# New places for the pieces of eight batches in the order lists of four engines

## The chip, the cores and the metric

The kernel runs on one core of one Trainium2 chip. The metric is device time in microseconds (us), the median of the runs; lower is better. The core's engines work through instruction lists of their own, in order, and meet at semaphores: TensorE (PE), VectorE (DVE), ScalarE (ACT), GpSimd (POOL) and SyncE (SP), which here only issues DMAs.

## What is computed

Eight batches of 512 rows with 256 features, in float32, pass through an attention block and a feed-forward block with experts:

```python
x = x + layernorm(attention(layernorm(x)))      # 16 heads of 16
x = x + layernorm(ffn(layernorm(x)))            # 8 experts, width 1024

# attention: the softmax weights are summed against the row's own v
att = softmax(einsum('blhd,bmhd->blmh', q, k) * scale, axis=2)
opt = einsum('blmh,blhd->blhd', att, v)
# ffn: the expert of a row is the argmax of its gate logits
base = x @ wi.T + wi_b
out = sum over i of (expert == i) * (relu(base + lora_i(x)) @ wo.T + wo_b)
```

In this form of attention a row's weights are summed over the keys before they meet v, so all that is needed of the 512x512 scores of a head is the exponentials' sum (divided by itself). The kernel still computes all scores, their maxima and exponentials.

## The kernel before

**Pieces.** A batch has 16 heads of 512 queries in four tiles of 128: 64 scores of 128x512. Score i is one matmul into one of NS = 5 PSUM banks `ps` (line 227); DVE takes its row maximum (`maximum`, line 735); ACT takes the exponential in place, with its sum (`exponential`, line 523). Score i waits until exponential i - 5 is done, since it uses its bank. The three remaining banks `pu` go round among all other pieces: `take` gives the next bank and waits until the last user of it has been evicted.

Around the scores lie, for batch b + 1: statistics (`x_stats`, DVE) and norm of x (`x_norm`, POOL), its transposes (`x_t`), the projections q, k (`q_k`, four pieces of six matmuls, in the order 0, 2, 1, 3) and v (`value`); each product is of float32 numbers split in a high and a low part, three matmuls. ACT evicts the high part, DVE forms the low one. For batch b - 1: the ratio of the sums (`ratio`, `ratio_whole`, DVE), `scale` of v (POOL), `o_t`, `project`, `y_stats`, `y_norm`, `sum_stats`, `sum_norm`, `y_t`, the gate (`gate`, `gate_t`, `logits`, `gate_1` to `gate_3`, `mask`, `masked_t`) and the first products of the feed-forward block, `f1` (eight pieces; f1_lows on POOL splits the first six, f1_last on DVE the last two). For batch b - 2: the end of f1, `f2` (eight pieces of twelve matmuls), `y2_bias`, `y2_stats`, `y2_norm`, and the store.

**Order.** The order is written out by hand. In each engine's function, `slot(s)` stands for score s + 4 on the PE, maximum s + 2 on DVE and exponential s on ACT, and the other pieces stand between the slots. Before the change one list serves batches 0 to 6 (pieces of batches that don't exist do nothing) and one serves batch 7, where the second half of the rows is finished in halves (`o_half`, `y_half`, `gate_half`, `f1_half`, `f2_last`) after the last score. In batches 0 and 1 the PE runs one idle matmul on `ones_r` (line 206) ahead of each score whose number isn't in FULL.

**Transfers.** q and k of each head have to lie on other partitions for the scores: `stacks(b, j)` on SP issues eight DMAs from qk to `stack` (line 1202) for piece j, a quarter of a batch, into a ring of three; `first_piece` does so in halves at the start, on SP and POOL. q_k(b + 1, 0) on ACT waits until all stacks of batch b have landed, for it overwrites qk. In batch 0 SP also loads weights in stages into buffers used otherwise later: it waits for late 4 (POOL has split the first half of wi), then issues the second half of wi, the lora weights and stacks(0, 2), waits for late 12 (wo split), then issues x of batches 2 and 3 and stacks(0, 3).

```python
            for b in range(B):
                if b:
                    stacks(b, 3)
                store(b - 3)
                load_x(b + 2 if b >= 2 else B)
                stacks(b + 1, 0), stacks(b + 1, 1), stacks(b + 1, 2)
```

## Time and profile before

| | us |
|---|---|
| median of 3 runs | 535.78 (535.15 to 537.13) |
| span of the profiled execution | 533.9 |
| DVE, ACT, POOL busy in it | 467.3, 454.1, 344.7 |
| PE busy, modelled | 509.3 |
| exponential 0 of batch 0 | 23.25 |
| exponential 0 of batches 1, 2 and 7 | 72.02, 132.33, 427.41 |

The span begins with the first instruction. Matmuls overlap and their ends are modelled, so a busy PE isn't a full one. "Idle before <- releaser" in a timeline row is the time that the engine stood still ahead of the instruction, and what released it. In a chain row a piece is on the path that ended last; ACT's exponentials count there as two instructions each, the exponential and the read of its sum.

### The profile page before, as it was taken

The page shows a single profiled execution, that of the slowest core. Times are in us where ns is not written, and L with a number is a line of the kernel's source. Part 1 is how long each engine was busy: PE and PEld are TensorE (multiplying, and loading weights), DVE is VectorE, ACT ScalarE, POOL GpSimd, SP SyncE. Part 2 cuts the span into 40 slices and gives each one's busy share as a digit, 9 for nine tenths or more (in the row PEclk, how much of TensorE's full clock was granted, in tenths as well). Part 3 has the DMA queues.
Part 4 walks back from the last instruction along what each step waited for, and adds up shares of the span by engine and source line. Part 5 has one row for each costly group of instructions (what it writes and reads, how often), then busy time and mean ns, then how long its engine had stood idle before and what let it go on. Part 6 is the DMA issues. An engine that isn't in the chain of part 4 may idle for free.

```text
span 533.9 us, 8929 instructions
## 1 busy us (share of the span) xinstructions
PE 509.3 (95%) x2752; PEld 412.8 (77%) x2752; DVE 467.3 (88%) x1005; ACT 454.1 (85%) x1238; POOL 344.7 (65%) x544
## 2 busy tenths in 40 slices
PE   8899989899999999999999999999999999899995
PEld 6666645688897779877897779877887778677995
...
GB/s 233 194 239 112 95 143 80 1 34 170 63 89 1 146 93 152 6 68 170 50 111 1 160 79 158 1 100 137 111 9 16 174 163 5 80 41 1 1 40 41
DMA packets 22691, 47.63 MB, mean 89 GB/s; under 512 B 5266, under 2 KB 13586, under 8 KB 22004
## 3 DMA queue, kind: packets, MB, share of 16 engines
...
q0 software_dynamic: 256, 0.52, 0.4%
q8 instruction: 22, 0.36, 0.3%
q10 hardware_dynamic: 432, 0.59, 0.3%
q14 instruction: 25, 0.20, 0.1%
...
## 4 chain that ended last, share of the span: by engine, by line
PE 52%; ACT 30%; POOL 6%; SPq 4%; DVE 3%; issue 2%; DMA 1%; POOLq 0%; ACTq 0%
PE pu L199 25%; ACT ps L523 22%; PE ps L227 10%; PE pu L283 5%; SPq L1202 3%; ACT y L590 3%; PE pu L239 3%; PE ps L199 2%; PE ps L206 2%; POOL y L1032 2%; DMA stack<-qk 1%; POOL nmr L1026 1%; PE pu L305 1%; ACT qk L537 1%; POOL xb L1038 1%
## 5 line engine op out<-in xcount | busy, mean ns | idle before, releaser
L523 ACT ACTIVATE ps<-ps,nmax 128x512 f32<-128x512 f32 x512 | 346.2, 705 | 19.8 <-DVE nmax L735 19.6
L735 DVE TENSOR_REDUCE nmax<-ps 128x1 f32<-128x512 f32 x512 | 324.5, 681 | 25.9 <-PE ps L227 24.3
L227 PE MATMUL ps<-stack 128*128 128x512 f32 x512 | 186.7, 420 | 2.3 <-ACT ps L523 1.6
L523 ACT ACTIVATION_READ_ACCUMULATOR ps<-ps,nmax 128x1 f32 x512 | 129.4, 253 | 0.0
L227 PEld LDWEIGHTS ps<-stack 128*128 128x128 f32 x512 | 93.5, 190 | 27.1 <-ACT ps L523 12.5
L199 PEld LDWEIGHTS pu<-wo_r,inter 128*128 128x128 f32 x744 | 95.4, 188 | 3.8
L199 PE MATMUL pu<-wo_r,inter 128*128 128x256 f32 x744 | 97.2, 282 | 0.0
L199 PE MATMUL pu<-yT,wi_r 128*128 128x512 f32 x336 | 87.4, 395 | 0.0
L199 PEld LDWEIGHTS pu<-yT,wi_r 128*128 128x128 f32 x336 | 63.2, 188 | 14.0 <-ACT xn L590 0.2
L206 PE MATMUL ps<-ones_r 128*128 128x512 f32 x132 | 55.1, 459 | 7.7 <-ACT ps L523 6.5
L1046 POOL TENSOR_TENSOR ml<-gs,g 128x128 f32<-128x128 f32 (+1 forms) x9 | 3.5, 387 | 77.9 <-DVE g L887 77.9
L199 PE MATMUL pu<-xnT,wqk_r 128*128 128x512 f32 x192 | 49.6, 396 | 0.8 <-DVE xnT L739 0.7
L206 PEld LDWEIGHTS ps<-ones_r 128*128 128x128 f32 x132 | 26.4, 202 | 30.7 <-ACT ps L523 24.4
L1103 POOL TENSOR_TENSOR inter<-y,inter 128x1024 fp32r<-128x1024 f32 x19 | 45.4, 2390 | 1.5
L199 PEld LDWEIGHTS pu<-xnT,wqk_r 128*128 128x128 f32 x192 | 35.5, 188 | 10.0 <-ACT y L635 1.2
L1026 POOL TENSOR_TENSOR nmr<-nmr,halves 128x2 f32<-128x2 f32 (+2 forms) x50 | 39.8, 797 | 4.2
L1038 POOL TENSOR_TENSOR xb<-xb,y 128x256 f32<-128x256 f32 x58 | 41.1, 735 | 1.8
L1069 POOL TENSOR_TENSOR vo<-vo,sone 128x256 f32<-128x256 f32 x32 | 18.9, 622 | 30.8 <-DVE sone L838 26.5
L283 PE MATMUL pu<-wout_s,oT 128*128 128x256 f32 x120 | 31.2, 384 | 3.1 <-ACT oT L551 2.1
L1023 POOL TENSOR_SCALAR nmr<-mv 128x2 f32<-128x2 f32 (+2 forms) x50 | 12.0, 240 | 34.0 <-DVE mv L782 30.9
L1032 POOL TENSOR_SCALAR y<-y,nmr 128x256 f32<-128x256 f32 x58 | 31.6, 555 | 2.4
L283 PEld LDWEIGHTS pu<-wout_s,oT 128*128 128x128 f32 x120 | 22.1, 189 | 9.4 <-issue 5.4
...
## 6 DMA issues: line engine op xcount, KB each, us to landing
stack<-qk SPq DMA_DIRECT2D x256, 128.0 KB, 2.5
...
```

The lines of the kernel that those rows point to most:

```text
L199: p = e.matmul(out_, lT(a, c), r(b_, c), start=first and n == 0 and j == 0, stop=last and n == len(chunks) - 1 and j == 2)
L206: e.matmul(bank[:].rearrange("p (k m) -> p k m", k=4), ones_r[:], ones_r[:].unsqueeze(1).to_broadcast([128, 4, 128]), start=True, stop=True)
L227: e.matmul(ps[i % NS][:], st[:, 1 - p, c, t * 128:(t + 1) * 128], st[:, 2, c, :], start=True, stop=True).then_inc(scored, 1)
L239: p = e.transpose(bank[:, t * 128:(t + 1) * 128], src[:, t, c * 128:(c + 1) * 128], id_s[:])
L283: p = e.matmul(o, oT[:, c, t * 128:(t + 1) * 128], wout_s[:, c, :], start=c == 0, stop=c == 1)
L523: e.activation(ps[i % NS][:], ps[i % NS][:], ACT.Exp, bias=nmax[:, i % 8:i % 8 + 1], accum_out=ssum[:, b % 2, t, h:h + 1]).then_inc(exped, 1)
L735: e.tensor_reduce(nmax[:, i % 8:i % 8 + 1], ps[i % NS][:], AX_X, ALU.max, negate=True).then_inc(maxed, 1)
L1026: e.tensor_tensor(nmr[n][:, 2, s], nmr[n][:, 1, s], halves[:, s], ALU.pow).then_inc(rstd[i], 1)
L1032: e.tensor_scalar(dst[:, t, :], src[:, t, :], nmr[n][:, 0, t:t + 1], nmr[n][:, 2, t:t + 1], ALU.add, ALU.mult).then_inc(normed[i], 1)
L1038: e.tensor_tensor(xb[:, b % XB, t, :], xb[:, b % XB, t, :], src[:, t, :], ALU.add).then_inc(added[i], 1)
L1069: e.tensor_tensor(vt, vt, sone[:, t, :].unsqueeze(2).to_broadcast([128, H, 16]), ALU.mult).then_inc(scaled, 1)
L1103: e.tensor_tensor(inter[:, 1, f:f + 2, :], whole, high.bitcast(F32), ALU.subtract).then_inc(f1_pool_low, 1)
```

## The change

The order lists of PE, ACT and DVE are written out anew, as four: batch 0, batch 1, batches 2 to 6, and batch 7. POOL has batch 1 apart. No piece is added or left out but one idle matmul (FULL has 30 numbers, not 31). Some moves: in middle batches f1(b - 1, 4) is evicted at the start of the next batch; f2 starts four scores later; q_k(b + 1, 3) goes from slots 40, 43 and 44 to slots 46, 49 and 49 of PE, ACT and DVE; in batch 0, x_t(1, .) comes earlier and value(1, .) and q_k(1, 3) later. x_stats(1) stands ahead of the first maximum, and x_norm(1) ahead of the splits of wi and wo on POOL. Four waits for loaded weights go from the start of batch 1 to the pieces that read them: wout_loaded to project(0, 0), late to gate(0), lora_moved to f1(0, 0), bg_loaded to gate(0) on ACT. SP's list is unchanged.

The old lists, which the diff takes away, are in the kernel above. Of the new ones the diff shows those of PE, ACT and DVE for the middle batches, the start and parts of batches 0, 1 and 7, and POOL's.

```diff
 
 
-IDLE, FULL = (25, 6, 4), (20, 29, 32, 35, 38, 41, 43, 45, 68, 70, 71, 72, 74, 84, 90, 93, 96, 97, 99, 102, 105,
-                           107, 109, 111, 112, 113, 115, 120, 123, 126, 127)
+IDLE, FULL = (25, 6, 4), (8, 28, 32, 35, 39, 50, 53, 61, 69, 71, 73, 75, 76, 82, 84, 90, 96, 98, 99, 100, 102, 103,
+                           105, 107, 109, 112, 115, 117, 121, 126)
 NS = 5
...
             def project(b, t):
                 if here(b):
                     u, k = divmod(t, 2)
+                    if b == 0 and t == 0:
+                        e.wait_ge(wout_loaded, 16)
...
                     bank = banks[take(("gate", b), gT_here, b + 1)]
+                    if b == 0:
+                        e.wait_ge(late, LATE)
                     e.wait_ge(yT_low, 2 * b + 2)
...
                           (0, 1), True, False)
                     if f == 0:
+                        if b == 0:
+                            e.wait_ge(lora_moved, 16)
                         e.wait_ge(lt_here, b + 1)
...
@@ tensor @@
...
+            def slot(s):
+                score(2 * PAIRS * b + s + 4)
+
+            b = 0
+            slot(0), slot(1), slot(2), slot(3), slot(4), slot(5), slot(6), slot(7), x_t(b + 1, 0), x_t(b + 1, 1)
+            slot(8), slot(9), slot(10), slot(11), slot(12), slot(13), slot(14), slot(15), slot(16), slot(17)
+            slot(18), slot(19), slot(20), slot(21), slot(22), slot(23), slot(24), slot(25), slot(26), slot(27)
+            q_k(b + 1, 0), slot(28), slot(29), slot(30), slot(31), q_k(b + 1, 2), slot(32), slot(33), slot(34)
+            q_k(b + 1, 1), slot(35), slot(36), slot(37), slot(38), q_k(b + 1, 3), slot(39), slot(40), slot(41)
+            slot(42), slot(43), slot(44), slot(45), slot(46), slot(47), slot(48), slot(49), value(b + 1, 0)
+            slot(50), slot(51), slot(52), value(b + 1, 1), value(b + 1, 2), slot(53), slot(54), slot(55), slot(56)
+            slot(57), slot(58), slot(59), slot(60), value(b + 1, 3), slot(61), slot(62), slot(63)
+
...
+            for b in range(2, B - 1):
+                slot(0), slot(1), slot(2), f1(b - 2, 7), slot(3), slot(4), o_t(b - 1, 0), o_t(b - 1, 1), slot(5)
+                slot(6), slot(7), project(b - 1, 0), slot(8), slot(9), project(b - 1, 1), slot(10), slot(11)
+                project(b - 1, 2), project(b - 1, 3), slot(12), slot(13), slot(14), slot(15), f2(b - 2, 0, 0)
+                slot(16), f2(b - 2, 0, 1), slot(17), slot(18), f2(b - 2, 1, 0), slot(19), slot(20), f2(b - 2, 1, 1)
+                slot(21), slot(22), x_t(b + 1, 0), slot(23), x_t(b + 1, 1), slot(24), slot(25), f2(b - 2, 2, 0)
+                slot(26), slot(27), f2(b - 2, 2, 1), slot(28), slot(29), slot(30), f2(b - 2, 3, 0), slot(31)
+                slot(32), f2(b - 2, 3, 1), y_t(b - 1, 0), y_t(b - 1, 1), slot(33), slot(34), q_k(b + 1, 0), slot(35)
+                slot(36), gate(b - 1), slot(37), q_k(b + 1, 2), slot(38), slot(39), gate_t(b - 1), slot(40)
+                value(b + 1, 0), slot(41), value(b + 1, 1), slot(42), value(b + 1, 2), slot(43), q_k(b + 1, 1)
+                slot(44), slot(45), slot(46), value(b + 1, 3), q_k(b + 1, 3), slot(47), slot(48), slot(49)
+                masked_t(b - 1), slot(50), f1(b - 1, 0), slot(51), f1(b - 1, 1), slot(52), slot(53), f1(b - 1, 2)
+                slot(54), slot(55), slot(56), f1(b - 1, 3), slot(57), slot(58), slot(59), slot(60), f1(b - 1, 4)
+                slot(61), slot(62), f1(b - 1, 5), slot(63), f1(b - 1, 6)
+            b = B - 1
+            slot(0), slot(1), slot(2), f1(b - 2, 7), slot(3), o_t(b - 1, 0), o_t(b - 1, 1), slot(4), slot(5)
+            slot(6), project(b - 1, 0), project(b - 1, 1), slot(7), slot(8), slot(9), project(b - 1, 2), slot(10)
+            project(b - 1, 3), slot(11), slot(12), f2(b - 2, 0, 0), slot(13), f2(b - 2, 0, 1), slot(14), slot(15)
+            slot(16), slot(17), f2(b - 2, 1, 0), slot(18), slot(19), slot(20), f2(b - 2, 1, 1), slot(21)
+            f2(b - 2, 2, 0), slot(22), slot(23), slot(24), slot(25), f2(b - 2, 2, 1), slot(26), slot(27)
+            y_t(b - 1, 0), slot(28), y_t(b - 1, 1), slot(29), slot(30), f2(b - 2, 3, 0), gate(b - 1), slot(31)
+            slot(32), slot(33), gate_t(b - 1), f2(b - 2, 3, 1), slot(34), o_half(0), slot(35), slot(36), slot(37)
+            project(b, 0), slot(38), masked_t(b - 1), slot(39), project(b, 1), slot(40), slot(41), f1(b - 1, 0)
+            slot(42), slot(43), slot(44), f1(b - 1, 1), slot(45), f1(b - 1, 2), slot(46), slot(47), slot(48)
+            slot(49), f1(b - 1, 3), slot(50), slot(51), slot(52), f1(b - 1, 4), slot(53), slot(54), slot(55)
+            f1(b - 1, 5), slot(56), f1(b - 1, 6), slot(57), slot(58), slot(59), f1(b - 1, 7), f2(b - 1, 0, 0)
+            more_banks(), f2(b - 1, 0, 1), o_half(1), project(b, 2), project(b, 3), y_half(0), f2(b - 1, 1, 0)
+            f2(b - 1, 1, 1), gate_half(0), f2(b - 1, 2, 0), gate_t_half(0), f2(b - 1, 2, 1), f2(b - 1, 3, 0)
+            y_half(1), f2(b - 1, 3, 1), masked_t_half(0), gate_half(1), f1_half(0, 0), gate_t_half(1), f1_half(0, 1)
+            f1_half(0, 2), f1_half(0, 3), masked_t_half(1), f1_half(1, 0), f1_half(1, 1), f2_last(0), f1_half(1, 2)
+            f1_half(1, 3), f2_last(1), f2_last(2), f2_last(3)
 
...
 
             def gate(b):
                 if here(b):
+                    if b == 0:
+                        e.wait_ge(bg_loaded, 16)
...
@@ scalar @@
...
+            b = 0
+            slot(0), slot(1), slot(2), slot(3), slot(4), slot(5), slot(6), slot(7), slot(8), slot(9), slot(10)
+            slot(11), slot(12), slot(13), slot(14), x_t(b + 1, 0), x_t(b + 1, 1), slot(15), slot(16), slot(17)
+            slot(18), slot(19), slot(20), slot(21), slot(22), slot(23), slot(24), slot(25), slot(26), slot(27)
+            slot(28), slot(29), slot(30), slot(31), q_k(b + 1, 0), slot(32), slot(33), slot(34), slot(35)
+            q_k(b + 1, 2), slot(36), slot(37), slot(38), q_k(b + 1, 1), slot(39), slot(40), slot(41), slot(42)
+            slot(43), slot(44), slot(45), slot(46), slot(47), slot(48), slot(49), slot(50), slot(51), q_k(b + 1, 3)
+            slot(52), slot(53), slot(54), slot(55), slot(56), slot(57), slot(58), slot(59), slot(60), slot(61)
+            slot(62), slot(63), value(b + 1, 0), value(b + 1, 1)
...
+            for b in range(2, B - 1):
+                f1(b - 2, 4), slot(0), slot(1), f1(b - 2, 5), slot(2), f1(b - 2, 6), slot(3), slot(4), slot(5)
+                slot(6), f1(b - 2, 7), o_t(b - 1, 0), o_t(b - 1, 1), slot(7), slot(8), slot(9), slot(10), slot(11)
+                slot(12), slot(13), slot(14), slot(15), slot(16), slot(17), slot(18), slot(19), slot(20), slot(21)
+                slot(22), slot(23), slot(24), f2(b - 2, 0), slot(25), slot(26), slot(27), x_t(b + 1, 0), slot(28)
+                slot(29), x_t(b + 1, 1), slot(30), slot(31), slot(32), slot(33), slot(34), f2(b - 2, 1)
+                y_t(b - 1, 0), y_t(b - 1, 1), slot(35), slot(36), q_k(b + 1, 0), slot(37), slot(38), gate(b - 1)
+                slot(39), q_k(b + 1, 2), slot(40), slot(41), logits(b - 1), slot(42), slot(43), value(b + 1, 0)
+                gate_exp(b - 1), slot(44), slot(45), slot(46), q_k(b + 1, 1), slot(47), value(b + 1, 1), slot(48)
+                slot(49), q_k(b + 1, 3), masked_t(b - 1), slot(50), slot(51), f1(b - 1, 0), slot(52), slot(53)
+                slot(54), slot(55), f1(b - 1, 1), slot(56), slot(57), slot(58), slot(59), slot(60), f1(b - 1, 2)
+                slot(61), f1(b - 1, 3), slot(62), slot(63)
...
@@ vector @@
...
+            x_stats(1)
             maximum(0), maximum(1)
...
+            slot(28), slot(29), slot(30), slot(31), slot(32), slot(33), slot(34), slot(35), q_k(b + 1, 0), slot(36)
+            slot(37), slot(38), q_k(b + 1, 2), slot(39), slot(40), slot(41), slot(42), slot(43), slot(44), slot(45)
+            slot(46), slot(47), slot(48), slot(49), slot(50), slot(51), q_k(b + 1, 1), slot(52), slot(53)
...
+            b = 1
+            ratio(b - 1), slot(0), ratio_whole(b - 1), slot(1), slot(2), slot(3), x_stats(b + 1), slot(4), slot(5)
...
+            for b in range(2, B - 1):
+                slot(0), ratio(b - 1), x_stats(b + 1), ratio_whole(b - 1), slot(1), slot(2), slot(3), slot(4)
+                f1_last(b - 2, 6), slot(5), slot(6), f1_last(b - 2, 7), slot(7), slot(8), slot(9), slot(10)
+                slot(11), project(b - 1, 0), slot(12), y_stats(b - 1, HALVES[0]), slot(13), slot(14)
+                project(b - 1, 1), slot(15), slot(16), y_stats(b - 1, HALVES[1]), slot(17), slot(18), slot(19)
+                slot(20), slot(21), slot(22), sum_stats(b - 1, HALVES[0]), slot(23), slot(24), slot(25), slot(26)
+                sum_stats(b - 1, HALVES[1]), slot(27), slot(28), slot(29), slot(30), slot(31), x_t(b + 1, 0)
+                slot(32), slot(33), x_t(b + 1, 1), y2_stats(b - 2, HALVES[0]), slot(34), y_t(b - 1, 0)
+                y_t(b - 1, 1), slot(35), slot(36), slot(37), q_k(b + 1, 0), slot(38), slot(39), slot(40), slot(41)
+                q_k(b + 1, 2), slot(42), gate_1(b - 1), slot(43), slot(44), gate_2(b - 1), slot(45), gate_3(b - 1)
+                slot(46), slot(47), q_k(b + 1, 1), y2_stats(b - 2, HALVES[1]), slot(48), slot(49), q_k(b + 1, 3)
+                slot(50), slot(51), slot(52), slot(53), slot(54), slot(55), slot(56), slot(57), slot(58), slot(59)
+                slot(60), slot(61), slot(62), slot(63)
...
+            norm(2, 1, y, xb[:, b % XB], b, HALVES[1]), gate_half(3, 0), y_half(1), gate_half(1, 1), gate_half(2, 1)
+            gate_half(3, 1), f1_half(0, 0), f1_half(0, 1), f1_half(0, 2), f1_half(0, 3), y2_stats(b - 1, HALVES[0])
+            y2_stats(b - 1, HALVES[1]), f1_half(1, 0), f1_half(1, 1), f1_half(1, 2), f1_half(1, 3), last_stats(0)
+            norm(3, 2, y2, y2, b, (0,)), last_stats(1), add(3, y2, b, (0,)), last_stats(2), last_stats(3)
+            norm(3, 2, y2, y2, b, (1,)), norm(3, 2, y2, y2, b, (2,)), add(3, y2, b, (1,)), add(3, y2, b, (2,))
+            norm(3, 2, y2, y2, b, (3,)), add(3, y2, b, (3,))
 
 
...
@@ pool @@
...
             e.wait_ge(normed[0], 4)
             first_piece(e, 0, 1)
             first_piece(e, 1, 1)
+            x_norm(1)
             late_halves(0, [(wi_r[:, :, 0, half(i)], wi_st[:, half(i)]) for i in range(2)], wi_loaded, 16)
             late_halves(4, [(wo_r[:, :, 2 * i:2 * i + 2], wo_st[:, 2 * i:2 * i + 2]) for i in range(4)], wo_loaded, 16)
-            x_norm(1)
             late_halves(12, [(wi_r[:, :, 1, half(i)], wi_st[:, half(i)]) for i in range(2)], wi_loaded, 32)
...
-            for b in range(1, B - 1):
+            b = 1
+            scale(b - 1), x_norm(b + 1), v_bias(b), y_norm(b - 1, HALVES[0]), y_norm(b - 1, HALVES[1])
+            sum_norm(b - 1, HALVES[0]), sum_norm(b - 1, HALVES[1]), mask(b - 1), f1_lows(b - 1, 0, 0)
+            f1_lows(b - 1, 0, 1)
+
+            for b in range(2, B - 1):
                 scale(b - 1), f1_lows(b - 2, 1, 0), x_norm(b + 1), y_norm(b - 1, HALVES[0])
                 y_norm(b - 1, HALVES[1]), sum_norm(b - 1, HALVES[0]), sum_norm(b - 1, HALVES[1]), y2_bias(b - 2, 0)
                 v_bias(b), y2_bias(b - 2, 1), mask(b - 1), y2_norm(b - 2), f1_lows(b - 1, 0, 0)
                 f1_lows(b - 1, 0, 1)
             b = B - 1
-
             scale(b - 1), f1_lows(b - 2, 1, 0), y_norm(b - 1, HALVES[0]), y_norm(b - 1, HALVES[1])
-            sum_norm(b - 1, HALVES[0]), sum_norm(b - 1, HALVES[1]), y2_bias(b - 2, 0), v_bias(b), scale_half(0)
+            sum_norm(b - 1, HALVES[0]), sum_norm(b - 1, HALVES[1]), v_bias(b), y2_bias(b - 2, 0), scale_half(0)
             y2_bias(b - 2, 1), mask(b - 1), y2_norm(b - 2), y_norm(b, HALVES[0]), f1_lows(b - 1, 0, 0)
-            f1_lows(b - 1, 0, 1), sum_norm(b, HALVES[0]), scale_half(1), f1_lows(b - 1, 1, 0)
-            spread(1, 1, b, HALVES[1]), spread(2, 1, b, HALVES[1]), mask_half(0), y2_bias(b - 1, 0)
-            mask_half(1), y2_bias(b - 1, 1), y2_norm(b - 1), spread(3, 2, b, (0,)), spread(3, 2, b, (1,))
-            spread(3, 2, b, (2,)), spread(3, 2, b, (3,))
-
+            f1_lows(b - 1, 0, 1), f1_lows(b - 1, 1, 0), scale_half(1), sum_norm(b, HALVES[0])
+            spread(1, 1, b, HALVES[1]), spread(2, 1, b, HALVES[1]), mask_half(0), mask_half(1), y2_bias(b - 1, 0)
+            y2_bias(b - 1, 1), y2_norm(b - 1), spread(3, 2, b, (0,)), spread(3, 2, b, (1,)), spread(3, 2, b, (2,))
+            spread(3, 2, b, (3,))
```

## Rows read from the trace of the kernel before

**Rows 1.** Busy table by stretch; batches 0, 1, 4 and 7.

```profile
23.25:72.02 48.77, 45.54 (x175) 28.61 (x174) 46.40 (x80) 47.07 (x136) 26.55 (x33) 0.97 0.62 156
72.02:132.33 60.31, 55.67 (x254) 41.26 (x254) 53.96 (x114) 54.87 (x152) 29.12 (x47) 1.00 0.30 74
250.50:309.47 58.97, 58.20 (x322) 48.28 (x321) 55.86 (x121) 56.11 (x156) 41.79 (x65) 1.00 0.34 90
427.41:485.20 57.79, 53.85 (x289) 43.56 (x288) 52.31 (x114) 52.71 (x149) 45.76 (x72) 1.00 0.25 66
```

**Rows 2.** Chain of the work that ended last, batch 4: start, us, what.

```profile
255.06 0.98 ACT oT L551 x2
...
256.18 1.10 PE pu L283 x4
...
285.41 0.83 PE pu L305 x8
...
297.25 4.01 ACT ps L523 x12
```

**Rows 3.** Timeline of ACT in batch 4: start, us, instruction, [idle before <- releaser].

```profile
261.25 0.66 ACT L523 ACTIVATE ps<-ps,nmax 128x512 f32<-128x512 f32 x1 [0.54 <-DVE nmax L735]
...
267.88 0.66 ACT L523 ACTIVATE ps<-ps,nmax 128x512 f32<-128x512 f32 x1 [0.46 <-DVE nmax L735]
...
270.73 0.60 ACT L529 ACTIVATE xnT<-pu 128x512 fp32r<-128x512 f32 x1 [0.25 <-PE pu L239]
...
286.27 0.30 ACT L568 ACTIVATE gs<-pu 128x160 f32<-128x160 f32 x1 [0.29 <-PE pu L305]
```

**Rows 4.** Timeline of DVE at the start of batch 4.

```profile
249.05 1.40 DVE L777 BATCH_NORM_STATS2 st<-xb 128x6 f32<-128x256 f32 x4
...
250.77 0.52 DVE L833 RECIPROCAL srec<-ssum 128x64 f32<-128x64 f32 x1
...
251.47 1.88 DVE L735 TENSOR_REDUCE nmax<-ps 128x1 f32<-128x512 f32 x3
253.27 0.68 DVE L767 SCALAR_TENSOR_TENSOR inter<-pu,inter 128x512 fp32r<-128x512 f32 x1
...
259.62 0.74 DVE L777 BATCH_NORM_STATS2 st<-y 128x6 f32<-128x256 f32 x2
...
260.56 0.66 DVE L735 TENSOR_REDUCE nmax<-ps 128x1 f32<-128x512 f32 x1
```

**Rows 5.** Timeline of ACT in batch 0 and at the start of batch 1.

```profile
26.15 0.66 ACT L523 ACTIVATE ps<-ps,nmax 128x512 f32<-128x512 f32 x1 [1.45 <-DVE nmax L735]
...
47.55 0.69 ACT L537 ACTIVATE qk<-pu,bqk_s 128x512 fp32r<-128x512 f32 x1 [0.25 <-DMA stack<-qk]
...
74.91 0.66 ACT L523 ACTIVATE ps<-ps,nmax 128x512 f32<-128x512 f32 x1 [1.23 <-DVE nmax L735]
```

**Rows 6.** Timeline of POOL in batch 0.

```profile
22.10 1.18 POOL L1125 CAST wi_r<-vo 128x512 fp32r<-128x512 f32 x2
...
25.69 2.27 POOL L1125 CAST wo_r<-xb 128x512 fp32r<-128x512 f32 x4
...
33.02 0.24 POOL L1023 TENSOR_SCALAR nmr<-mv 128x4 f32<-128x4 f32 x1
...
36.94 1.17 POOL L1125 CAST wi_r<-vo 128x512 fp32r<-128x512 f32 x2
```

**Rows 7.** Timeline of the SP queue in batch 0: DMA issues.

```profile
28.39 0.58 SPq L1225 DMA_DIRECT2D vo<-in_wi  x1
...
59.44 0.59 SPq L1202 DMA_DIRECT2D stack<-qk  x1
```

**Rows 8.** Chain of the work that ended last, at 40 us.

```profile
40.68 6.71 DMA stack<-qk
```

**Rows 9.** Line 1202, stack transfers on SP, late in batch 4.

```profile
L1202 SPq DMA_DIRECT2D stack<-qk x11: 547/592/601, 293.8 to 300.4; - x11
...
DMA to landing us min/median/max: 2.3/2.4/2.6
```

290 lines of the change are left out of this document (65 added, 225 removed).

## The prediction

> **Names and clock of the argument.** Exponential k, maximum k and score k of a batch are its k-th of 64; slot s of the PE list holds score s+4, of the DVE list maximum s+2, of the ACT list exponential s. Times in a batch count from the start of its exponential 0.
>
> **What bounds the kernel now.** I read the busy table by batch first [rows 1], then the chain of the work that ended last inside a middle batch [rows 2], then the timelines of ACT and DVE there [rows 3, 4], then the start [rows 5 to 8] and the stack transfers [rows 9]. In rows 1 the reader is to see that no engine is far ahead: in batch 4 (58.97 us) ACT is busy 56.11, DVE 55.86 and the PE 58.20, a modelled figure. Batches 2 to 6 run from 132.33 to 427.41 [rows 1], 59.0 each. Exponentials end at 485.20; 48.7 us of tail follow.
>
> The chain [rows 2] shows what closes a middle batch: ACT evicts o_t until 256.04, and from 256.18 to 286.24 the chain is on the PE without a break (project, eight f2 groups, transposes, q_k, gate, gate_t); then it is ACT's to the end. ACT waits on both neighbours: for late maxima at 261.25 and 267.88, the first and the last of four such waits, behind the project additions and statistics on DVE; and for the PE at 270.73 and 286.27, two of four small ones [rows 3]. All lists are in order and five score banks tie them: score k+5 needs exponential k done. So what a new order can win is waits, no work.
>
> **The middle batches, 2 to 6.** The number of instructions stays. Unit prices on DVE [rows 4]: x_stats 1.72 (249.05 to 250.77), ratio with ratio_whole 0.70, a maximum 0.60 (251.47 to 253.27 for three), a subtraction, projection or split about 0.60 too, one half of y_stats or sum_stats 0.94 (259.62 to 260.56). An exponential starts 0.7 after its maximum starts (260.56 and 261.25) [rows 3, 4]. On ACT an exponential costs 0.67 (4.01 for six with their reads), a plain eviction 0.49 (0.98 for two) [rows 2].
>
> Maximum 19, old: x_stats is already over, both halves of y_stats and the first of sum_stats are ahead; exponential 19 starts 17.38 into the batch (267.88) [rows 1, 3]. New: ratio can start when exponential 63 has ended, 0.25 before the new exponential 0 (f1(4) now stands between). Ahead of maximum 19 come 0.70 + 1.72 + sixteen maxima 9.6 + two f1_last 1.2 + two projections 1.2 + two halves of y_stats 1.88 = 16.3, so it starts at 16.05 and exponential 19 at 16.75: 0.63 earlier. Both halves of sum_stats are now behind it.
>
> From there to the next exponential 0 ACT has the same 45 exponentials and the same evictions, old and new. Old, this leg took 41.59, with four waits for the PE; each shows as idle before its row (0.25, 0.29 in rows 3) and the four are worth 1.07 when spacing is taken against unit price. New, I carry both lists forward with the same prices: DVE is late for exponentials 25, 29 and 37 by 0.1, 0.22 and 0.36, 0.68 in all. The difference is 0.4. The PE: its unbroken leg from project to gate_t was 30.06 [rows 2]; the new one has one q_k fewer and two scores more, and gate_t's reader, logits, moved from before exponential 37 to before 42. Starting at 7.25 the leg ends at about 36.4, and ACT reaches logits at 37.2; so the PE no longer sets ACT's time there, by 0.8. Its other groups end 0.1 to 1 us before ACT wants them; f1(6) and the first f1 of the next batch are the thin ones (0.1 to 0.3). A middle batch comes to 58.97 - 0.63 - 0.4 = 57.9 to 58.0, so -1.0 each and -1.2 in batch 2: **-5.2 for the five**. Bounds: if the thin margins all fail, old waits return (0); if also the small unexplained spacing goes, 57.2 (-1.8 each).
>
> POOL, in order, follows: scale 2.4 to 4.9, last f1_lows to 8.4 (the projection on DVE that waits for it comes at 10), y_norm to 20.5, sum_norm to 26.5, before y_t at 28.9. Nothing queues behind it.
>
> **Batch 0.** Old, x_stats(1) stands behind maximum 1, and exponential 2 waits, idle 1.45 at 26.15 [rows 5]; 1.57 is lost. New it stands ahead of maximum 0, where DVE waits for scores anyway: free. But that gain meets a transfer. ACT's q_k(1,0) waits until stacks(0,1) to (0,3) have landed, since it overwrites what they read; old it goes at 47.55, released by a DMA [rows 5] that landed at 47.39 [rows 8]. ACT now is there at about 45.7 and waits. And the landing moves: x_norm(1) on POOL, 3.92 long (33.02 to 36.94), goes ahead of the weight splits that began at 22.10. The fourth of them, at 25.69 old [rows 6], is what SP waits for (late 4); SP was there at 28.39 [rows 7]. New it comes at 29.6, and behind that wait stand on SP the second wi load, the lora loads, stacks(0,2), two x loads and stacks(0,3). So 1.25 late, landing at 48.6. From q_k(1,0) on the work is the same (24.47 to the next exponential 0): 73.1. A second transfer adds to that: q_k(1,3) moves from slots 43/44 to slots 51/53 on ACT and DVE, so the stack for score 64 is issued at about 65.0, not 59.44 [rows 7], and needs 7.1 (eight issues of 0.59, then 2.4) [rows 9]: 72.1. Score 64 precedes value(1,3) on the PE, whose eviction precedes exponential 64: 73.6 against 72.02. **+1.6**, bounds 0 (the landing doesn't move) and +3.5.
>
> By the row, SP's issue and the DMA both count: the last piece took 6.71 to land at 40.68 [rows 8], against 2.3 to 2.6 in a middle batch [rows 9], so there is a backlog. The Trainium skill ("DMA: Bandwidth & Descriptors", Issuing engines are not separate DMA queues) says that transfers of all issuers share sixteen engines and interleave, and that the issuing matters little beside them. By that rule alone the landing would stay near 47.4 and batch 0 would cost 0.4 where I take 1.6.
>
> **Batch 1.** Old, exponential 2 at 74.91 waited for maximum 2 behind x_stats and ratio, idle 1.23, 1.57 lost [rows 5]. New, ratio comes first and x_stats behind slot 3. Carried forward with the same prices, DVE sets ACT's time until exponential 36 (DVE's x_t, projections and statistics stand closer together), ACT alone after it: 57.3, and with the 0.6 of small gaps that old batches show beside such a sum 57.9 against 60.31 [rows 1]: **-2.4**, bounds -3.2 and -0.8. The waits for late, wout_loaded, lora_moved and bg_loaded cost nothing at either place: POOL, whose late pieces set the last of them, had finished these long before batch 1 and idled for ratio; behind the old ones stood the PE's score 4, behind the new ones project, gate, f1 and gate on ACT. If a load were late it would have cost o_t too, since scale waits for v_bias. One idle matmul more of 0.23 lies in the PE's waits for ACT.
>
> **Last batch and tail.** Batch 7 has no x_t, q_k and value; ACT is busy 52.71 of 57.79 [rows 1], so 4 to 5 of waits are there. The same carrying forward leaves four of them on maxima (17, 20, 38, 39) and one on logits, about 3.5 in all: **-1.0**, bounds +0.5 and -1.8. In the tail the PE has nearly the whole chain. f2(0,1) now fills the time in which POOL scales the second half, and project 2 and 3 follow o_half(1) at once, so y_half(1), at the end of the longest chain, comes about 1 earlier; at the very end norm and add of tiles 1 and 2 stand ahead of norm of tile 3 (+0.3). **-1.0**, bounds +0.7 and -2.
>
> **Sum.** +1.6 - 2.4 - 5.2 - 1.0 - 1.0 = -8.0. The profiled execution has a span of 533.86; the median of the runs is 535.78, 1.9 more, which stays. 535.8 - 8.0 = 527.8.
>
> **Rivals.** (A) The PE's waits come back: the middle batch won 0.4 + 0.63 on paper, with PE margins of 0.1 to 0.3, and the two-engine sum of ACT and DVE alone is no smaller than the old one (57.2 against 56.9). What the old order lost to the PE, 2.07 a batch, would be lost again: 59.3 a batch, +1.6 in place of -5.2: 534.6. For it: the PE was the chain for 30 us; against it: logits moved off its leg. 0.20. (B) Slower: the stack for score 64 binds in every batch. q_k(b+1,3) on DVE ends at 46.5 instead of about 43.2 (SP issues at 293.8, 43.3 into the batch); eight issues and 2.4 give 53.6 [rows 9], and the PE wants score 64 at 53.5. Each us beyond costs nearly one, five times. It decides from a landing about 1.6 later than 53.6, where the gain of -8.0 is eaten; at the landing times of the start (6.7 in place of 2.4 [rows 8, 9]) it would be 4 late: 547. Against it: no x load or store stands near. 0.11. (C) The small spacing goes too, 57.2 a batch, batch 1 at 57.3, tail -1.8: 522.6. 0.14. (D) Rule of the shared engines: landing unmoved, 526.6; it lies in the forecast's range. 0.05. Forecast: 0.50.
>
> **How the numbers follow.** Faster by over 0.5% (below 533.1) holds the forecast, C and D, 0.69; within 0.5% (about what a measurement of this kernel can tell from no change) is A, 0.20 less a little, 0.19; slower 0.12. The range leaves out B and the far half of C: 522.5 to 536.
>
> **What would show it.** After: exponential 2 of batch 0 0.7 behind exponential 1; q_k(1,0) on ACT waiting for a DMA for 2 to 3.5; exponential 64 near 73.6; middle batches 57.9 apart, exponential 19 at 16.75, no wait of ACT at logits; q_k(b+1,3)'s stack landed just as score 64 is due. Wrong if middle batches stay at 59, with ACT idle behind the PE, or if score 64 waits for a stack.

## The result and the profile after

The changed kernel takes 529.62 us (median of 4 runs, 529.12 to 530.09) against 535.76 (535.15 to 537.13): ratio 0.988, 95% interval 0.9862 to 0.9898. The forecast was 527.8 with a range of 522.5 to 536.0. The sign and the range held and the total lies nearest to the likeliest case, but partly by luck: of the five terms of the sum only batch 1's came near in this execution, and the errors of the others partly cancelled. Below, "old" and "changed" are the two kernels, and a batch runs from its exponential 0 to the next one's.

| stretch of the profiled execution | old, us | changed, us | forecast change | measured change |
|---|---|---|---|---|
| start to exponential 0 of batch 1 | 72.02 | 74.77 | +1.6 | +2.8 |
| batch 1 | 60.31 | 58.09 | -2.4 | -2.2 |
| batches 2 to 6 | 295.08 | 286.94 | -5.2 | -8.1 |
| batch 7, exponential 0 to 63 | 57.05 | 58.58 | -1.0 | +1.5 |
| tail from exponential 63 | 49.40 | 49.61 | -1.0 | +0.2 |
| span | 533.86 | 527.99 | -8.0 | -5.9 |

The busy table by stretch of the changed kernel, the columns of rows 1 (stretch, length; PE, PEld, DVE, ACT, POOL busy; granted clock, DMA share, GB/s): batches 0, 1, 4, 7, tail.

```profile
23.12:74.77 51.65, 46.02 (x173) 27.75 (x172) 43.77 (x71) 47.27 (x136) 26.89 (x32) 0.96 0.52 138
74.77:132.86 58.09, 56.14 (x249) 41.56 (x249) 53.52 (x112) 54.45 (x150) 26.33 (x46) 0.97 0.34 85
248.21:305.39 57.18, 56.49 (x321) 48.15 (x320) 55.19 (x121) 55.66 (x155) 41.77 (x65) 1.00 0.34 89
...
419.80:478.38 58.58, 56.40 (x302) 45.75 (x301) 54.74 (x117) 53.61 (x150) 47.33 (x69) 1.00 0.30 79
478.38:527.99 49.61, 41.61 (x339) 40.46 (x337) 24.20 (x76) 10.47 (x24) 23.13 (x49) 0.97 0.07 22
```

Against rows 1 the reader is to see two things: batch 4 is 1.8 shorter with about the same work, and batch 1 has a granted clock of 0.97 where it had 1.00. Batch 0 is below full in both, 0.96 and 0.97: in the old kernel the clock is low from 28.8 to 32.1, in the changed one from 71.1 on. Batch 7's stretch in rows 1 ends 0.74 behind exponential 63; here it ends at its start, so lengths go by the table.

**The middle batch.** The chain of the work that ended last in batch 4 (start, length, what), to be laid beside rows 2:

```profile
254.57 0.98 ACT oT L533 x2
255.69 1.10 PE pu L285 x4
...
276.23 1.44 PE pu L199 x12
277.68 0.60 ACT y L619
278.28 0.95 ACT yT L538 x2
...
295.71 2.66 ACT ps L505 x8
```

In rows 2 the chain stayed on the PE from project for 30 us, to gate_t, and came back to ACT at the logits (286.27). Now it comes back 22.0 after project, when ACT evicts f2 (L619), and then runs on ACT without a break to o_t's eviction in the next batch. The waits that are left show in ACT's timeline, of which the first row is the eviction of o_t: late maxima at exponentials 15, 17 and 19, and f2.

```profile
254.28 1.26 ACT L533 ACTIVATE oT<-pu 128x512 f32<-128x512 f32 x2
...
261.17 0.66 ACT L505 ACTIVATE ps<-ps,nmax 128x512 f32<-128x512 f32 x1 [0.28 <-DVE nmax L692]
...
262.96 0.66 ACT L505 ACTIVATE ps<-ps,nmax 128x512 f32<-128x512 f32 x1 [0.34 <-DVE nmax L692]
...
265.08 0.66 ACT L505 ACTIVATE ps<-ps,nmax 128x512 f32<-128x512 f32 x1 [0.67 <-DVE nmax L692]
...
277.68 0.60 ACT L619 ACTIVATE y<-pu 128x512 f32<-128x512 f32 x1 [0.19 <-PE pu L199]
```

These legs close over one batch: from the eviction of o_t to project 1.4 (254.28 to 255.69), from project to f2's eviction 22.0 (277.68), from f2's eviction on ACT to the next batch's o_t 33.8 (220.5 in batch 3 to 254.28): 57.2, the length of the batches 3 to 6 (57.25, 57.18, 57.21, 57.19). Any legs that close over a batch add up to its length; that these bind is read from the chain, which follows them without a break. The PE's leg binds by a little only: ACT waited 0.19 at f2, so a shorter PE leg alone would win about that much (an estimate from this row), and ACT would then be held by the late maxima before. There is no wait at the logits, and exponential 19 starts 16.87 into the batch.

**Batch 0.** PE's timeline at the stack transfer for score 64, and the PE by microsecond there (stretch, length, busy and matmuls; granted clock, DMA share, GB/s):

```profile
71.74 0.80 PE L206 MATMUL ps<-ones_r 128*128 128x512 f32 x1 [2.96 <-DMA stack<-qk]
72.33 0.63 PE L227 MATMUL ps<-stack 128*128 128x512 f32 x1
72.76 1.49 PE L199 MATMUL pu<-wv_r,xnT 128*128 128x256 f32 x6
```

```profile
70.00:71.00 1.00, 0.00 (x0) 1.00 0.83 205
71.00:72.00 1.00, 0.26 (x1) 0.57 0.81 213
72.00:73.00 1.00, 1.00 (x4) 0.50 0.83 205
```

The PE has nothing to do for 2.96 us, and where it starts again the granted clock is 0.50, the lower of its two levels (1.2 GHz); it is 0.51 still from 77 to 78, and 1.00 from 78 on.

Batch 0 is the stretch that differs most from one execution to the next, so one trace is a poor measure of it. Eight traces have the changed lists there (the changed kernel, e4 to e8, e11, e12): batch 0 took 50.04 to 52.20, mean 51.1, and exponential 64 stood at 72.94 to 75.30, mean 74.1. The old lists took 48.77, and 48.70 in e3. In all eight the PE idled 2.94 to 3.20 ahead of score 64 and the clock fell to 0.50 near the end of that gap or up to 1.4 behind it, for 3.4 us in seven traces and for 6.8 in this one.

**Into batch 7.** VectorE's timeline, then POOL's, then the PE's, around exponential 0 of batch 7 (419.80):

```profile
420.66 1.21 DVE L795 TENSOR_TENSOR sone<-ssum,srec 128x64 f32<-128x64 f32 x1
```

```profile
419.38 2.40 POOL L1039 TENSOR_TENSOR inter<-y,inter 128x1024 fp32r<-128x1024 f32 x1
```

```profile
417.07 0.50 PE L227 MATMUL ps<-stack 128*128 128x512 f32 x1 [0.68 <-DMA stack<-qk]
```

ratio_whole (L795) takes 0.19 in batches 3 to 6; here 1.21, and it ends 0.09 after POOL's f1_lows does. The transfer is late by one issue: line 1141 (durations of an issue in ns: least, median, longest; then first and last start), whose longest issue is 1648 ns where the median is 592.

```profile
L1141 SPq DMA_DIRECT2D stack<-qk x12: 547/592/1648, 409.1 to 417.2; - x12
```

### The profile page after: what moved, and what is told of

It is laid out like the page before. It is cut to its first block, busy times and chain, and to the rows that moved or that the text cites. A ratio compares the mean times of both kernels' runs of the same rounds, so it can differ in the third digit from the quotient of the medians.

```text
span 528.0 us, 8930 instructions
## 1 busy us (share of the span) xinstructions
PE 504.7 (96%) x2753; PEld 414.6 (79%) x2753; DVE 464.7 (88%) x1005; ACT 452.3 (86%) x1238; POOL 345.3 (65%) x544
## 4 chain that ended last, share of the span: by engine, by line
PE 44%; ACT 28%; DVE 21%; issue 2%; SPq 2%; DMA 1%; POOL 0%; POOLq 0%; ACTq 0%
ACT ps L505 20%; PE pu L199 20%; DVE nmax L692 12%; PE ps L227 9%; PE ps L199 4%; PE pu L285 4%; PE ps L206 3%; DVE st L734 2%; SPq L1141 2%; ACT y L574 2%; ACT qk L519 2%; PE pu L239 1%; ACT inter L568 1%; DMA stack<-qk 1%; DVE mv L739 1%
## 5 line engine op out<-in xcount | busy, mean ns | idle before, releaser
L692 DVE TENSOR_REDUCE nmax<-ps 128x1 f32<-128x512 f32 x512 | 321.2, 679 | 23.4 <-PE ps L227 22.3
L227 PE MATMUL ps<-stack 128*128 128x512 f32 x512 | 182.2, 416 | 1.2 <-DMA stack<-qk 0.7
L505 ACT ACTIVATION_READ_ACCUMULATOR ps<-ps,nmax 128x1 f32 x512 | 134.7, 263 | 0.0
L199 PEld LDWEIGHTS pu<-wo_r,inter 128*128 128x128 f32 x648 | 83.8, 188 | 4.2 <-POOL inter L1039 0.7
L199 PE MATMUL pu<-wo_r,inter 128*128 128x256 f32 x648 | 85.6, 282 | 0.5 <-DVE inter L724 0.5
L206 PE MATMUL ps<-ones_r 128*128 128x512 f32 x133 | 57.1, 472 | 8.3 <-ACT ps L505 4.0
L962 POOL TENSOR_TENSOR nmr<-nmr,halves 128x2 f32<-128x2 f32 (+2 forms) x50 | 39.7, 794 | 4.2
L285 PEld LDWEIGHTS pu<-wout_s,oT 128*128 128x128 f32 x128 | 23.5, 189 | 10.5 <-DVE inter L724 5.7
```

The costliest lines, as they stand in the source:

```text
L199: p = e.matmul(out_, lT(a, c), r(b_, c), start=first and n == 0 and j == 0, stop=last and n == len(chunks) - 1 and j == 2)
L206: e.matmul(bank[:].rearrange("p (k m) -> p k m", k=4), ones_r[:], ones_r[:].unsqueeze(1).to_broadcast([128, 4, 128]), start=True, stop=True)
L227: e.matmul(ps[i % NS][:], st[:, 1 - p, c, t * 128:(t + 1) * 128], st[:, 2, c, :], start=True, stop=True).then_inc(scored, 1)
L285: p = e.matmul(o, oT[:, c, t * 128:(t + 1) * 128], wout_s[:, c, :], start=c == 0, stop=c == 1)
L505: e.activation(ps[i % NS][:], ps[i % NS][:], ACT.Exp, bias=nmax[:, i % 8:i % 8 + 1], accum_out=ssum[:, b % 2, t, h:h + 1]).then_inc(exped, 1)
L692: e.tensor_reduce(nmax[:, i % 8:i % 8 + 1], ps[i % NS][:], AX_X, ALU.max, negate=True).then_inc(maxed, 1)
```

## Experiments

All start from the changed kernel, except e3. The kernel before, run beside them, took 535.7 to 536.0 (medians). "Middle batches" are 3 to 6. The cuts of code show the moved pieces alone.

**e1: the first batch's q_k readings early.** In batch 0 ACT evicts q_k(1,3) behind slot 41 (was 51), and DVE reads q_k(1,1) behind 40 and q_k(1,3) behind 43 (were 51 and 53).

```
-  slot(51), q_k(b + 1, 1), slot(52), slot(53), q_k(b + 1, 3), slot(54)
+  slot(40), q_k(b + 1, 1), slot(41), slot(42), slot(43), q_k(b + 1, 3), slot(44)
```

> The changed kernel, with the evictions of q_k(1, 3) on ACT moved from after slot 51 to after slot 41 of batch 0, and DVE's halves of q_k(1, 1) and q_k(1, 3) from after slots 51 and 53 to after slots 40 and 43. Theory (the stack transfer for score 64, issued at 64.8 and landed at 71.7, holds up the PE, and its clock falls in the wait): issue near 57.5, landing near 64.5, score 64 waits for no DMA, the granted clock stays at 1.0, batch 0 from exponential 0 to exponential 64 takes 48.9 instead of 51.65 and the time falls by 2.5 to 3, to about 526.9. Rival (the batch is long because of the wait at q_k(1, 0) for the last stack of batch 0): the time stays at 529.6.

525.82 us, ratio 0.9834 (0.9794 to 0.9874); three of its four runs took 525.5 to 525.9, one 529.55. Batch 0 fell from 51.66 to 49.04, and batch 1 from 58.09 to 56.51. SP issues the stack at 58.53, it lands at 66.23, score 64 follows at 69.41 with no wait, and the clock stays at full speed:

```profile
68.00:69.00 1.00, 1.00 (x4) 1.00 0.73 189
69.00:70.00 1.00, 0.96 (x7) 1.00 0.86 213
```

So the late place of q_k(1,3) costs some 3.8 us in all, more than half of what the change gained. e9 and e10 have the same edit: the three traces have 48.3 to 49.0 for batch 0 and 56.5 for batch 1, against means of 51.1 and 57.8 in those with the late place, 2.5 and 1.3.

**e2: idle matmuls while the PE waits for that stack.** Twelve of them ahead of score 64; the late transfer stays.

```
+  if i == 2 * PAIRS:
+      e.wait_ge(exped, i - NS + 1)
+      run_idle(ps[i % NS], 12)
```

> The changed kernel with 12 idle matmuls on the PE ahead of its wait for the stack of score 64. It takes away the idle time, not the wait. If the fall of the granted clock to 0.5 from 71.4 on is a cost of its own (value(1, 3) and the scores behind it at half speed), the clock stays at 1.0, exponential 64 comes 0.7 to 1.1 earlier than 74.77 and the time falls by about as much. If the wait for the landing alone sets it: no change.

529.41 us, ratio 0.9883 (0.9868 to 0.9898): no gain that the time shows. In the trace the clock is 1.00 from the landing on and, from there to exponential 64, 2.02 us passed where the changed kernel needed 3.08; value(1,3)'s six matmuls took 0.87 where they took 1.49. But the gap alone doesn't cost 1.06 each time: the same stretch took 2.03 to 3.08 in the eight traces without the idle matmuls, 2.5 in the mean, according to when the clock fell. Batch 1 took 57.43 here, 57.62 to 58.09 in those of the eight with the same list. So the clock's price is 0.5 in batch 0 and 0.4 in batch 1 by the means, and 1.1 and 0.7 in the changed kernel's own trace; it is read from traces, and the time doesn't confirm it. Of e1's 1.3 in batch 1, about 0.9 has other causes that were not parted.

Two other things lengthened the trace of e2, which is that of its slowest run (530.39). The pieces before landed at 48.30, not 47.36; the PE stood still for 2.44 ahead of 49.87, the clock was at 0.50 from 49.5 to 52.9 in spite of the edit further on, and the stack landed at 73.26, not 71.69. And in batch 4 one issue of the transfer took 1.42, the PE waited for the stack (last row below), and batch 5 took 58.03 instead of 57.21.

```profile
72.00:73.00 1.00, 1.00 (x6) 1.00 0.84 221
...
73.88 0.87 PE L199 MATMUL pu<-wv_r,xnT 128*128 128x256 f32 x6
...
302.50 0.50 PE L230 MATMUL ps<-stack 128*128 128x512 f32 x1 [0.69 <-DMA stack<-qk]
```

**e3: the new middle lists alone.** Batches 2 to 6 have the new lists on PE, ACT and DVE in the old kernel; f1(b-2,4) is evicted at the start of batch 7.

> The kernel before with the new lists of PE, ACT and DVE in batches 2 to 6 alone; at the borders f1(b - 1, 4) is evicted at the start of batch 2 and of batch 7 instead of the end of batches 1 and 6. If the whole gain sits in the middle batches (57.2 instead of 58.97 each), the time is 535.8 - 1.1 - 4 x 1.78 = 527.5, faster than the changed kernel. If their gain hangs on the new lists around them, it is above 530.

529.95 us, ratio 0.9889 (0.9874 to 0.9903). Missed by 2.4: batches 3 to 5 took 57.24, 57.19 and 57.29, but batch 6 took 59.07 and the tail 50.99 where either kernel has 49.4 to 49.6. Batch 6 behaves as in e4, and batch 7 took 56.97; why the tail was 1.5 longer stays open.

**e4: batch 7's old lists, on all four engines, behind the new middle ones.**

> The changed kernel with the old lists of batch 7 on all four engines. Theory (the new list of batch 7 is worse by itself: ratio_whole on DVE meets POOL's split of f1, and the additions at the end stand ahead of the last norm): 528.0, 1.5 less in batch 7 and 0.2 less in the tail. Rival (batch 7 is slower because the middle batches hand over later pieces, above all the stack that lands 0.7 late): no better than 529.3.

528.95 us, ratio 0.9872 (0.9851 to 0.9893), not to be told from the changed kernel. Batch 7 took 57.02 as in the old kernel, but batch 6 took 59.01: together 116.03, against 115.77 changed and 116.02 old. So the new lists of batch 7 are no worse than the old ones: with either, what batch 6 gained is gone at exponential 63 of batch 7, but for 0.3 at most. The PE's rows between its scores 0 and 63 of batch 7, old kernel, changed kernel and e4:

```profile
L199 PE MATMUL pu<-yT,wi_r 128*128 128x512 f32 x60 | 15.6, 395 | 0.0
```

```profile
L199 PE MATMUL pu<-yT,wi_r 128*128 128x512 f32 x66 | 17.1, 395 | 0.0
```

```profile
L199 PE MATMUL pu<-yT,wi_r 128*128 128x512 f32 x66 | 17.2, 395 | 0.0
```

The middle lists hand one piece of f1 more to batch 7, six products. That alone isn't its length, for e4's batch 7 has them too and took 57.02. What e4 lacks is the changed order on ACT, which evicts 22 pieces between exponentials 0 and 63 where the old kernel and e4 evict 19: f1(5,5), which the old order has ahead of exponential 0, and f1(6,6) and f1(6,7), which it has behind exponential 63. From exponential 0 to 63 ACT is busy 53.61 instead of 51.97 and idle 5.0 instead of 5.1: the 1.5 is work, not waiting.

**e5: q_k(b+1,3) two slots later on DVE, middle batches.**

```
-  slot(49), q_k(b + 1, 3), slot(50), slot(51), slot(52)
+  slot(49), slot(50), slot(51), q_k(b + 1, 3), slot(52)
```

> In the middle batches DVE's q_k(b+1,3) is given out after slot 51 instead of slot 49, some 1.2 us later; nothing else is moved. The stack for score 64 landed 53.6 us into batch 4 of the changed kernel and score 64 stood at 53.64: if the transfer has no slack left, as the rival with the late stack says, score 64 waits about 1.2 us in each middle batch, the batches go from 57.2 to 58.2 to 58.4 and the whole to 534 to 536. Theory of slack further on (ScalarE wants score 64 only some 2.5 us after it): TensorE waits in the trace, but the middle batches stay at 57.2 to 57.4 and the whole at 529.6 to 530.5.

534.38 us, ratio 0.9968 (0.9957 to 0.9979); middle batches 58.2 to 58.5. That is what a transfer without slack was to give, and not what the theory of slack was. But the PE had two new waits, one of them for the bank that q_k(b+1,3) holds until DVE has read it; the second row is PEld's.

```profile
355.82 0.96 PE L199 MATMUL pu<-yT,wi_r 128*128 128x512 f32 x3 [0.74 <-DVE qk L706]
...
362.75 0.19 PEld L227 LDWEIGHTS ps<-stack 128*128 128x128 f32 x1 [0.36 <-DMA stack<-qk]
```

**e12: only the transfer later.** This parts the two.

```
+  if j == 0 and 3 <= b:
+      e.wait_ge(maxed, 2 * PAIRS * (b - 1) + 54)
```

> SyncE alone is held: the first stack of the next batch is issued when maximum 53 is done, about 1.2 us after q_k(b+1,3) instead of at once, for batches 3 to 7; VectorE reads the bank of q_k when it did. It parts the two costs of e5, where TensorE also waited 0.71 us for that bank. Theory (no slack in the transfer): score 64 comes 1.1 us late, middle batches take 58.2, the whole 534. Rival (most of e5's loss was the wait for the bank, and the late stack is partly made up, since ScalarE wants exp 64 only 3.6 us after score 64): middle batches 57.3 to 57.8, the whole 530 to 532.

534.02 us, ratio 0.9962 (0.995 to 0.9974); batches 58.21 to 58.45. SP issues it 1.3 behind q_k's end, and each of the four batches is 1.0 to 1.3 longer. The PE waits for it each time, 0.86 to 1.12, as here in batch 5:

```profile
362.00 0.50 PE L227 MATMUL ps<-stack 128*128 128x512 f32 x1 [0.90 <-DMA stack<-qk]
```

The stack has next to no slack in the changed kernel, where it lands 53.4 to 53.6 into batches 3 to 5 and score 64 of batch 4 stands at 53.64: the rival of the late stack had its mechanism right, and the changed kernel stands at its edge. The way to ACT is the f1 pieces behind score 64: ACT waits up to 0.6 for them and evicts o_t 7.08 into the batch instead of 6.06, so the whole loop starts later.

**e11: less TensorE work in the second half of a batch.**

```
-  (0, 1), True, False)
+  (0,) if f in (1, 2) and 1 <= b <= B - 3 else (0, 1), True, False)
```

> The pieces 1 and 2 of the feed-forward's first layer, f1(b-1,1) and f1(b-1,2) in the middle batches, leave out half of their products (3 of 6 matmuls each), so 1.4 us of TensorE work a batch is gone and nothing of the other engines; those batches' output is incomplete. Theory (TensorE bounds the middle batches): a middle batch falls from 57.2 to 56.2 or less, the next bounds being ScalarE's 55.7 busy and VectorE's 55.2; the whole to about 525. Rival (the chain between VectorE and ScalarE, or the transfer of the stack, sets the batch): 57.2, 529.6 unchanged.

Two pieces of f1 leave out half of their products in the middle batches. 529.8 us, ratio 0.9877 (0.986 to 0.9895); middle batches 57.18 to 57.25. The theory that TensorE's work in this half bounds them falls; its leg from project to f2 was not touched. The PE's 1.4 us turned into waiting, part of it for the same stack:

```profile
359.23 0.50 PE L227 MATMUL ps<-stack 128*128 128x512 f32 x1 [0.30 <-DMA stack<-qk]
```

**e8: x_stats a batch ahead.** Middle batches lose 1.7 us of DVE work between ratio and maximum 3; it is done behind slots 55 and 58 of the batch before.

```
-  slot(0), ratio(b - 1), x_stats(b + 1), ratio_whole(b - 1), slot(1)
+  slot(0), ratio(b - 1), ratio_whole(b - 1), slot(1)
+  ... slot(55), x_stats(b + 2, HALVES[0], False), slot(56), slot(57), slot(58), x_stats(b + 2, HALVES[1])
```

> The statistics of the next batch's input, 1.7 us of VectorE work between ratio and maximum 1 of every middle batch, are done in the batch before, in two halves behind slots 55 and 58. Theory (VectorE's leg from ratio to maximum 19 sets when exp 19 starts, and that sets the batch): exp 19 of a middle batch starts 15.1 us into it instead of 16.9 and the batch takes 55.8 to 56.5, the whole 523 to 525. Rival (the time is only moved, since VectorE and ScalarE are also late in the second half of the batch, or TensorE is near its bound): exp 19 is earlier, but a wait at slots 56 to 63 takes its place, batches stay at 57.2, the whole at 529 to 530.

530.64 us, ratio 0.9903 (0.9877 to 0.993); middle batches 57.1 to 57.5. The time isn't won, but the reason is neither of the two: exponential 19 came at 16.78, hardly earlier, since ratio_whole now met POOL's f1_lows and took 1.48 instead of 0.19, 1.3 of the 1.7 that the move was to save. DVE's row, then POOL's, which ends 0.08 before it (303.74 + 2.40 = 306.14; 304.74 + 1.48 = 306.22):

```profile
304.74 1.48 DVE L799 TENSOR_TENSOR sone<-ssum,srec 128x64 f32<-128x64 f32 x1
```

```profile
303.74 2.40 POOL L1044 TENSOR_TENSOR inter<-y,inter 128x1024 fp32r<-128x1024 f32 x1
```

**e6: ratio_whole of batch 7 behind slots 0 and 1.**

```
-  ratio(b - 1), ratio_whole(b - 1), slot(0), slot(1), slot(2)
+  ratio(b - 1), slot(0), slot(1), ratio_whole(b - 1), slot(2)
```

> In batch 7 alone, VectorE's ratio_whole stands behind slots 0 and 1. Theory (it took 1.21 us instead of 0.2 since POOL's f1_lows was running beside it, and maximum 2 came late): the one operation takes 0.2 to 0.6, exp 2 doesn't wait, batch 7 goes from 58.6 to about 57.6 and the whole to 528.6. Rival (whichever VectorE operation stands there is drawn out, or ScalarE loses the same time at a later wait): batch 7 stays at 58.3 to 58.6, 529.6.

529.46 us, ratio 0.9878 (0.986 to 0.9896). ratio_whole took 0.22, at 420.89, but batch 7 took 58.55: unchanged. DVE waited 0.40 and 1.04 for the PE's scores instead:

```profile
420.89 0.22 DVE L795 TENSOR_TENSOR sone<-ssum,srec 128x64 f32<-128x64 f32 x1
422.14 1.29 DVE L692 TENSOR_REDUCE nmax<-ps 128x1 f32<-128x512 f32 x2 [1.04 <-PE ps L227]
```

Two causes stand side by side there, the PE late by the stack, and ratio_whole, and either is enough for the loss. In e2's trace the stack of batch 6 was on time and the PE didn't wait, ratio_whole took 1.72, and batch 7 took 58.54; here ratio_whole is short and the stack late (the PE waited 0.62), and it took 58.55. In e10, below, score 64 did not wait and ratio_whole took 0.60: 57.80. That fits, but e10 differs in more than that.

**e7: the old order of DVE's last list.** The changed kernel has both norms ahead of both adds, behind last_stats(3).

```
-  last_stats(2), last_stats(3), norm(3, 2, y2, y2, b, (1,)), norm(3, 2, y2, y2, b, (2,)), add(3, y2, b, (1,))
-  add(3, y2, b, (2,))
+  last_stats(2), norm(3, 2, y2, y2, b, (1,)), add(3, y2, b, (1,)), norm(3, 2, y2, y2, b, (2,)), last_stats(3)
+  add(3, y2, b, (2,))
```

> The end's last list on VectorE stands as in the kernel before (norm 1, add 1 and norm 2 ahead of the last statistics of tile 3), all else as changed. Theory (the new order puts norms and adds of tiles 1 and 2 ahead of norm 3, and POOL's spreads slow beside them): the time from last_stats(3) to the end goes from 3.6 back to 2.9, the whole to 528.9. Rival (last_stats(3) itself comes later by what then stands ahead of it): 529.6, unchanged, or up to 0.5 longer.

528.48 us, ratio 0.9858 (0.9838 to 0.9879). From last_stats(3) to the last add: 2.89 instead of 3.58, as the theory said; but last_stats(3) itself came 43.56 after exponential 63 instead of 43.12, as the rival said, since norm 2 waits 0.46 for POOL ahead of it. The tail took 49.36, 0.25 less: that is the net price of the new order. The old kernel's tail took 49.40, so what the change did ahead of the end won nothing in sum. The rest of the 1.1 of the medians is not the end's (batch 0 was 1.1 shorter in this trace). POOL's last spread (L960, then L962), changed kernel and e7:

```profile
523.05 0.91 POOL L960 TENSOR_SCALAR nmr<-mv 128x1 f32<-128x1 f32 x1
```

```profile
521.90 0.21 POOL L960 TENSOR_SCALAR nmr<-mv 128x1 f32<-128x1 f32 x1
```

**e9: e1 and a third order at the end.** Beside e1's edit:

```
+  last_stats(2), norm(3, 2, y2, y2, b, (1,)), add(3, y2, b, (1,)), last_stats(3), norm(3, 2, y2, y2, b, (2,))
+  add(3, y2, b, (2,))
```

> The first batch's q_k readings early (as in e1, which took 525.8), and a third order of the last list on VectorE: norm 1 and add 1 ahead of the last statistics of tile 3, norm 2 and add 2 behind them. Theory (norm 2 ahead of them made VectorE wait 0.46 us for POOL and the statistics 0.43 late; norm 2 with two adds behind them slowed POOL's spread): statistics of tile 3 start 43.1 us after exp 63, the end comes 3.3 after them, the tail is 48.9 instead of 49.6 and the whole about 525.1. Rival (any norm and add behind the statistics slows the spread as much): 525.8.

525.39 us, ratio 0.9795 (0.9777 to 0.9814), the fastest of all. The tail is 49.08: last_stats(3) at 43.11, 3.06 from there to the last add, L960 at 0.38. Against e1 (525.82) the total is within what two medians can differ by; the 0.55 of the tail is read from the traces.

**e10: e9 with e6's edit, and q_k(b+1,3) before slot 48 on ACT and DVE in the middle batches.**

> e9 with ratio_whole of batch 7 behind slots 0 and 1 and, in the middle batches, q_k(b+1,3) two places earlier on ScalarE and VectorE (before slot 48), so that each batch's stack has over 1 us to spare. Theory (middle batches are bound by TensorE, 56.65 of 57.19 us busy in the changed kernel, and the spare time helps only where an issue takes 1.65 us, ahead of batch 7): middle batches stay at 57.2, batch 6 and batch 7 together go from 115.8 to about 114.8, the whole to 524.1. Rival (the transfer binds each batch): middle batches go to 56.8 or less, the whole to 522 or less. Second rival (the last two batches and the end are bound by TensorE's work too): 525.1, unchanged against e9.

532.93 us, ratio 0.9936 (0.9913 to 0.9958). A miss, by my own edit: middle batches took 58.84 to 58.88. I had moved q_k(b+1,3) on two engines and left it on the PE, so ACT waited for it, in order, with its exponentials behind:

```profile
348.92 0.69 ACT L519 ACTIVATE qk<-pu,bqk_s 128x512 fp32r<-128x512 f32 x1 [0.97 <-PE pu L199]
...
351.78 0.60 ACT L562 ACTIVATE lt_r<-pu 98x512 fp32r<-98x512 f32 x1 [0.35 <-PE pu L317]
```

The edit, on both engines (here VectorE's):

```
-  slot(48), slot(49), q_k(b + 1, 3)
+  q_k(b + 1, 3), slot(48), slot(49)
```

What it tells is a price: the gaps on ACT, 1.09 and 0.47 counted from start to start, make 1.56, and the batch is 1.65 longer. ACT's leg from f2 to the next o_t has no slack, as the loop above says. Whether an earlier stack wins anything by itself was not shown (it landed 52.2 to 52.5 into these batches, beside a larger loss), nor was the PE's leg of the loop, from project to f2, shortened in any run; that part of the loop is read from the trace alone.

## Why the prediction was right, and where not

**Middle batches: mechanism right, size missed.** Exponential 19 was put at 16.75 and came at 16.87; the PE no longer sets ACT's time at the logits; score 64 stood at 53.6 as worked out. The term was -1.0 and measured -1.8. The step that failed is the comparison by differences: I subtracted 0.63 and 0.4 from the old 58.97, and so kept 0.7 of "small unexplained spacing" in the new batch. The same carrying forward gave 57.2 as a bare sum, which stood in the text as a bound and as the rival of 0.14; that was the measurement. In the busy tables ACT's idle time fell from 2.9 to 1.5 and its busy time from 56.1 to 55.7, so most of the 1.8 was waiting; how much of it was waiting on the PE was not parted. I also did not name the next late thing. It is f2's eviction, 0.19 late, and the loop through project, f2 and ACT of 57.2.

**Batch 0: near, with a term left out.** ACT waited 1.92 at q_k(1,0), a little less than forecast. I had the landing 1.25 late. SP issued the third piece 1.8 to 2.4 later than before, yet in the two profiled kernels it landed at 47.36 and 47.39 [rows 8]. Over all traces it landed at 46.4 to 48.3 with the new lists (twelve, mean 47.2) and at 45.66 and 47.38 with the old ones: 0.7 later by the means. So the weight of the issue was too high, and the rule of the Trainium skill ("DMA: Bandwidth & Descriptors", Issuing engines are not separate DMA queues), that the issuing matters little beside the shared engines, is nearer than it seemed; two old traces don't decide between them. The second transfer was seen (issue at 65.0, landing 72.1, exponential 64 at 73.6; measured 64.78, 71.69, 74.77). What was left out is that 2.96 us without work cost the PE its clock behind it. e2 shows this term in the trace, at 1.1 in this execution and 0.5 in the mean. The forecast of 73.6 lies inside the 72.94 to 75.30 of the eight traces, and 0.5 below their mean: over half of the miss here is this execution.

**Batch 1: right.** -2.4 against -2.2, though by two errors: the order won more (56.5 in e1), and the late stack took some back, in part by the clock.

**Batch 7: wrong in sign.** I carried its lists forward for their waits and took ACT's work between exponentials 0 and 63 as unchanged. It is three evictions more, one handed over by the middle lists and two drawn ahead of exponential 63; at 0.49 each [rows 2] that is 1.5, the whole of the rise over the old 57.05. That was to be had by counting, and was not counted. The waits were forecast at about 3.5; ACT's idle time is 5.0, as before (5.1); 0.7 of them is the loss at the start, which the late stack and ratio_whole beside POOL each cause alone (e2, e6).

**Tail: wrong.** y_half(1) came 0.4 earlier, not 1, and even that didn't reach the end: with the old order of the end (e7) the tail is that of the old kernel to 0.04. The two evictions taken out of it won nothing either; the chain there is the PE's. The order of the end cost 0.25, near the +0.3 forecast. What ate the 0.4 stays open.

**Rivals.** The late stack (slower, 0.11) was no mishap: its arithmetic was exact to 0.1, and e12 shows a delay of 1.3 costing 1.0 or more in each of four batches. There the issuing does matter: eight issues of 0.59 are two thirds of the way from q_k to the landing, so the rule of the Trainium skill, near the mark in the crowded first batch, would mislead in a middle one. The return of the PE's waits did not happen. The rival of 522.6 was right for the middle and wrong for batch 1, batch 7 and the tail. So the forecast's total held although its middle batches were the rival's: a gain of 2.9 more there met losses of 1.2, 0.2, 2.5 and 1.2 elsewhere.
